# Finding the 896 unused rows and sending zeros to them, in place of zeroing all 39 blocks of the first layer's second group

## The reference, cut to what matters

```python
logits = jnp.einsum('btd,ed->bte', X, routing_W) + expert_bias      # 8 experts
activation = jnp.sqrt(jax.nn.softplus(logits))
top_vals, top_idx = jax.lax.top_k(activation, 2)
combine = jnp.sum(jax.nn.one_hot(top_idx, 8) * top_vals[..., None], axis=-2)
hdn = jax.nn.silu(jnp.einsum('nd,edh->enh', Xf, rW1) + rb1[:, None, :])
y = jnp.einsum('enh,ehd->end', hdn, rW2) + rb2[:, None, :]
routed = jnp.einsum('ne,end->nd', combine, y)
return shared + routed
```

## Time and profile before

| | us |
|---|---|
| median of 3 runs | 814.96 (814.42 to 817.94) |
| the profiled execution, its own time | 822.08 |
| its span | 820.2 |
| busy in the span: PE, DVE, ACT, POOL | 749.1, 530.4, 489.3, 429.7 |

### The profile page before, as it was taken

How to read it: one execution, slowest core, us unless ns; L and a number is a source line. 1 busy time by engine, 2 the same in 40 slices (tenths; PEclk the granted TensorE clock), 3 DMA queues, 4 the chain that set the end, 5 groups by cost and what they waited for, 6 DMA issues and landing times.

```text
span 820.2 us, 16199 instructions
## 1 busy us (share of the span) xinstructions
PE 749.1 (91%) x4633; PEld 653.7 (80%) x4633; DVE 530.4 (65%) x1423; ACT 489.3 (60%) x1379; POOL 429.7 (52%) x399
## 2 busy tenths in 40 slices
PE   4799987889898499999999999789999999999996
PEld 3546635676776399999998988689999999999995
DVE  5687857552665488888889888776543343365454
ACT  2337735555676488888877787356555454454541
POOL 3000655564687958888545778544652445333220
PEclk9899999999999799999999999899999999999998
DMA  8999997787899943663610444633444434565457
GB/s 248 343 285 308 332 300 257 241 276 227 184 268 241 320 121 81 163 153 70 210 63 2 161 163 148 206 104 120 140 137 142 144 104 133 179 210 177 161 178 233
DMA packets 128745, 154.47 MB, mean 188 GB/s; under 512 B 10875, under 2 KB 118550, under 8 KB 127638
## 3 DMA queue, kind: packets, MB, share of 16 engines
q1 hardware_dynamic: 102896, 112.55, 44.7%
q0 software_dynamic: 18624, 34.29, 15.8%
q10 hardware_dynamic: 7142, 6.59, 2.4%
HBM read 77.39 MB, written 76.00 MB: 187 GB/s over the span
## 4 chain that ended last, share of the span: by engine, by line
PE 70%; DVE 8%; issue 5%; ACT 5%; POOL 5%; DMA 4%; DVEq 1%; another core or an unknown queue 0%; SPq 0%; POOLq 0%; ACTq 0%
PE psum L849 24%; PE psum L1164 9%; PE psum L1142 8%; PE psum L1236 7%; PE psum L1241 6%; PE psum L1237 6%; POOL X L718 4%; PE psum L1152 3%; PE psum L1252 3%; ACT pr L1549 2%; PE psum L1215 2%; DMA X<-yl_dram,slots_y 1%; DMA yk_dram<-ys,L 1%; PE psum L1037 1%; PE psum L942 1%
## 5 line engine op out<-in xcount | busy, mean ns | idle before, releaser
L771 POOL DMA_INDIRECT yk_dram<-ys,L x52 | 53.6, 1031 | 136.2 <-ACT ys L1641 136.0
L718 POOL DMA_INDIRECT X<-yl_dram,slots_y x64 | 101.0, 1578 | 31.9 <-issue 14.2
L690 POOL DMA_INDIRECT xs_dram<-N,slots x64 | 65.9, 1029 | 97.0 <-DVEq L1943 58.4
L1549 ACT ACTIVATE pr<-psum,nmx 128x64 f32<-128x64 f32 x512 | 108.4, 365 | 6.8 <-DVE nmx L2314 6.6
L1236 PE MATMUL psum<-whi,xTh 128*128 x284 | 103.9, 366 | 3.4 <-ACT xTh L1603 2.4
L2410 DVE TENSOR_TENSOR hs<-psum,hs 128x384 f32<-128x384 f32 x71 | 39.7, 559 | 87.4 <-PE psum L1241 45.2
L1237 PE MATMUL psum<-wlo,xTh 128*128 x284 | 96.0, 338 | 0.0
L759 POOL DMA_INDIRECT xs_dram<-N,slots x64 | 69.7, 1090 | 35.9 <-ACT ys L1641 19.1
L1241 PE MATMUL psum<-whi,xTl 128*128 x284 | 74.1, 342 | 1.5 <-DVE xTl L2433 1.4
L751 POOL TENSOR_TENSOR pr<-pr,sm 128x1024 f32<-128x1024 f32 x32 | 62.2, 1944 | 19.5 <-DVE sm L2321 17.3
L1633 ACT ACTIVATE hs<-psum 128x384 f32<-128x384 f32 x71 | 34.9, 492 | 49.0 <-PE psum L1241 36.7
(11 more groups left out here) (370 smaller groups left out, 2041.2 us busy)
## 6 DMA issues: line engine op xcount, KB each, us to landing
fx<-xs_dram SPq DMA_DIRECT2D x78, 130.0 KB
yl_dram<-fy SPq DMA_DIRECT2D x78, 128.0 KB
xs_dram<-fill SPq DMA_DIRECT2D x4, 2340.0 KB, 14.1
xs<-xs_dram SPq DMA_DIRECT2D x71, 130.0 KB
wlo<-in_L_ffn_W_dram SPq DMA_DIRECT2D x4, 1536.0 KB, 11.4
xs_dram<-cz SPq DMA_DIRECT2D x1, 5070.0 KB, 24.2
xs_dram<-cz SPq DMA_DIRECT2D x7, 650.0 KB
X<-in_x_dram SPq DMA_DIRECT2D x4, 1024.0 KB, 11.7
```

What stands on the lines that cost most here:

```text
L690: po.indirect_dma_start(XS, bass.IndirectOffsetOnAxis(ap=slot[k][:, t:t + 1], axis=0), N0[:, t, :], None).then_inc(s[done], 16)
L718: po.indirect_dma_start(X[:, t, :], None, YL[b // 2], bass.IndirectOffsetOnAxis(ap=slot_y[k][:, t:t + 1], axis=0), compute_op=ALU.add).the ...
L771: po.indirect_dma_start(YK, bass.IndirectOffsetOnAxis(ap=yid[:, j:j + 1], axis=0), ys[j % YB], None).then_inc(s[f"y_out{j % YB}"], 16)
L1549: last = act(pr[b][:, S * h:S * h + S], bank[2 * b + h // 8][:, S * (h % 8):S * (h % 8) + S], ACT.Exp, bias=nmx[:, h:h + 1])
```

## The change

Group 1's rows are no longer filled. GpSimd writes the numbers 0, 128, ..., 768 plus the partition's into `pad_no` once, at the start. Behind `choose(1)` VectorE runs `padding()`, which finds for each of the 896 numbers which expert's open rows it falls to and writes the row in `pad_at`. Behind the 32 sends of group 1, GpSimd sends 128 rows of zeros 7 times by that list. SP waits for these too before it issues `vraw` and group 1's loads. The stores of `st_r` share semaphores two by two.

```diff
+PADS = LS - 2 * LT
@@ tiles
+        pad_no, pad_at = nmx[:, 0:PADS], sm[0][:, 0:PADS].bitcast(I32)
@@ SP
-            parts = [LS * i // PAIRS for i in range(PAIRS + 1)]
-            sp.dma_start(rows_of[0], zeros.to_broadcast([P, LS, XW])).then_inc(s["zeroed0"], 16)
+            sp.dma_start(XS[0:LS * P, :].rearrange("(p r) d -> p r d", p=P), zeros.to_broadcast([P, LS, XW])).then_inc(s["zeroed"], 16)
...
-                                     ...).then_inc(s[f"st_out{i}{j % DEEP}"], 16)
+                                     ...).then_inc(s[f"st_out{i // 2}{j % DEEP}"], 16)
-                sp.dma_start(rows_of[1][:, parts[j]:parts[j + 1], :],
-                             zeros.to_broadcast([P, parts[j + 1] - parts[j], XW])).then_inc(s["zeroed1"], 16)
...
                 if g:
+                    sp.wait_ge(s["padded"], 16 * PADS)
                     sp.dma_start(vraw, VD[0].rearrange("p (m c) n -> p m (c n)", c=2)).then_inc(s["v_in"], 16)
@@ GpSimd
+            po.iota(pad_no, pattern=[[P, PADS]], base=0, channel_multiplier=1, allow_small_or_imprecise_dtypes=True)
@@ GpSimd, send_rows(g)
-                po.wait_ge(s[f"zeroed{g}"], 16 * (1, PAIRS)[g])
+                if g == 0:
+                    po.wait_ge(s["zeroed"], 16)
...
+                if g:
+                    po.wait_ge(s["pads"], 1)
+                    for i in range(PADS):
+                        po.indirect_dma_start(
+                            XS, bass.IndirectOffsetOnAxis(ap=pad_at[:, i:i + 1], axis=0),
+                            zero4, None).then_inc(s["padded"], 16)
@@ VectorE, called between choose(1) and routed(0)
+            def padding():
+                base, e_ = LS * P, E * LT
+                counts, cum, open_, at = (ta[:, 2 * E * k:2 * E * k + E] for k in range(4))
+                at = at[:, 0:PADS]
+                c3 = wk12[:, 0:PADS * E].rearrange("p (i e) -> p i e", e=E)
+                last_t = tc_[:, e_:2 * e_].rearrange("p (e t) -> p e t", e=E)[:, :, LT - 1:LT]
+                nc.vector.tensor_copy(counts.rearrange("p (e a) -> p e a", a=1), last_t)
+                ve.drain()
+                nc.vector.tensor_tensor_scan(cum, ones8[:, :], counts, 0.0, ALU.mult, ALU.add)
+                ve.drain()
+                tt(cum, counts, cum, ALU.subtract)
+                ve.drain()
+                stt(open_, te[:, :], float(P), cum, ALU.mult, ALU.add)
+                ve.drain()
+                tt(c3, bc(pad_no, E), rep(open_, PADS), ALU.is_ge)
+                ve.drain()
+                tt(c3, c3, rep(counts, PADS), ALU.mult)
+                ve.drain()
+                nc.vector.tensor_reduce(at, c3, AX.X, ALU.add)
+                ve.drain()
+                stt(pad_at, at, float(base), pad_no, ALU.add, ALU.add)
+                ve.drain()
+                ve.sem_inc(s["pads"], 1)
@@
             choose(1)
+            padding()
             routed(0)
```

More of the change, by code:

```diff
@@ L307, in build @@
         VD = nc.dram_tensor("vw_dram", [NB, P, PAIRS, D], F32).ap()
-        names = """consts ctx_in u_in x_in0 x_in1 x_in2 x_in3 s_in0 s_in1 s_in2 s_in3 wq_in kvo_in w_in0 w_in1 w_in2 w_in3 w_hi w_lo cols_in rest_in cw_in l1_in zeroed0 zeroed1
+        names = """consts ctx_in u_in x_in0 x_in1 x_in2 x_in3 s_in0 s_in1 s_in2 s_in3 wq_in kvo_in w_in0 w_in1 w_in2 w_in3 w_hi w_lo cols_in rest_in cw_in l1_in zeroed pads padded
             u_c_in mid_in
-            pre_c_tp pre_c_sb wqt_p wqt_sb k_p k_sb v_p v_sb a_p vw_p st_sb st_out00 st_out01 st_out02 st_out10 st_out11 st_out12 st_out20 st_out21 st_out22 st_out30 st_out31 st_out32
+            pre_c_tp pre_c_sb wqt_p wqt_sb k_p k_sb v_p v_sb a_p vw_p st_sb st_out00 st_out01 st_out02 st_out10 st_out11 st_out12
             b2_in b2_lo b2_zero sw_in rw_in
@@ L416, in _ @@
             zeros = zero4[:, :].rearrange("p (a d) -> p a d", a=1)
-            rows_of = [XS[LS * P * g:LS * P * (g + 1), :].rearrange("(p r) d -> p r d", p=P) for g in range(LG)]
-            parts = [LS * i // PAIRS for i in range(PAIRS + 1)]
             sp.wait_ge(s["kvo_in"], 16 * 3)
@@ L438, in _ @@
                         sp.dma_start(AD[:, :, i, P * j:P * j + P].rearrange("b p n -> p b n"),
-                                     st_r[i][j % DEEP].rearrange("p (b n) -> p b n", b=NB)).then_inc(s[f"st_out{i}{j % DEEP}"], 16)
+                                     st_r[i][j % DEEP].rearrange("p (b n) -> p b n", b=NB)).then_inc(s[f"st_out{i // 2}{j % DEEP}"], 16)
                     else:
@@ L442, in _ @@
                         sp.dma_start(VD[2 * h:2 * h + 2, :, j, :].rearrange("b p n -> p b n"),
-                                     st_r[i][j % DEEP].rearrange("p (b n) -> p b n", b=2)).then_inc(s[f"st_out{i}{j % DEEP}"], 16)
-                sp.dma_start(rows_of[1][:, parts[j]:parts[j + 1], :],
-                             zeros.to_broadcast([P, parts[j + 1] - parts[j], XW])).then_inc(s["zeroed1"], 16)
-            for i in range(4):
+                                     st_r[i][j % DEEP].rearrange("p (b n) -> p b n", b=2)).then_inc(s[f"st_out{i // 2}{j % DEEP}"], 16)
+            for i in range(2):
                 for d in range(DEEP):
-                    sp.wait_ge(s[f"st_out{i}{d}"], 16 * len(range(d, PAIRS, DEEP)))
+                    sp.wait_ge(s[f"st_out{i}{d}"], 16 * 2 * len(range(d, PAIRS, DEEP)))
             for c in range(DC):
@@ L1382, in fold @@
                     if j >= DEEP:
-                        ac.wait_ge(s[f"st_out{i}{j % DEEP}"], 16 * (j // DEEP))
+                        ac.wait_ge(s[f"st_out{i // 2}{j % DEEP}"], 16 * 2 * (j // DEEP))
                     bk_, sc = (bank[2 + i], DH ** -0.5) if i < DC else (bank[3 + i], 1.0)
@@ L1424, in shared_out @@
                 elif q == 2:
-                    ac.wait_ge(s["st_out00"], 16 * len(range(0, PAIRS, DEEP)))
+                    ac.wait_ge(s["st_out00"], 16 * 2 * len(range(0, PAIRS, DEEP)))
                 for h, k in enumerate((6, (5, 4)[q // LQ])):
```

## The result

The changed kernel took 819.2 us (median of 20 runs), the kernel before 815.1 beside it. The ratio is 1.0058, with a 95% interval from 1.0037 to 1.0078: 4.7 us slower, 3.0 to 6.4. At 0.58% the slowdown lies just past the 0.5% up to which I had said "same" (chance 0.71), so in "slower" (0.23); its interval reaches to both sides of that line.

What follows compares the result with a forecast made beforehand. GpSimd's collects through `scale(0)` were taken as the bound. VectorE +1.03, GpSimd +1.35 and 0.2 for waits, with removal and SP at 0, made +2.6 us on 814.96: 817.6 us, range 812.5 to 821.0.

Steps and rivals of the forecast that it cites:

- Bound: GpSimd's collects of group 0 and `scale(0)`, 199.07 to 281.09 us, release TensorE's softmax turn; a late start ends late.
- Removal at 0: Dropping group 1's fill (5070 KB, 69 to 118 us) gains 0, since nobody on the chain waits for it.
- VectorE, +1.03: `padding()` ahead of `routed(0)` takes 2.12 us; block 0's copy, and the blocks' end, come 1.03 us later.
- The cover, TensorE's turn: VectorE's 1.09 us idle for TensorE's turn ahead of block 0's copy was to hide that much of `padding()`.
- GpSimd, +1.35: Seven sends behind group 1's last one take 8.82 us; what idle time doesn't cover delays the first collect by 1.35.
- the 7.78 idle us: GpSimd's idle time between its last send and the first collect, said to cover nearly all of the seven sends.
- slower collects: Rival: loads moving among the first eight collects lengthen two landing waits, 819.6 to 821.6 us; chance 0.15.
- SP's loads, 0: `vraw` goes out 7.1 us later, group 1's blocks start 1.0 to 4.0 us late; slack absorbs it, priced 0.
- this rival: Loads too late: group 1's late blocks use up the slack and GpSimd waits, 819.6 to 820.6 us; chance 0.08.
- the slack of 4.2: Group 1's blocks were done at about 262.8 us, 4.2 us before GpSimd passes their wait ahead of collect 33.
- Sum: Removal 0, VectorE +1.03, GpSimd +1.35 and 0.2 for waits, SP 0: +2.6 us, giving 817.6 us.

Runs made afterwards that it cites:

- run 1: Kernel before, fill kept, with `padding()` added ahead of `routed(0)` and its result unused: 1.0022, 817.88 us.
- run 9: Kernel before, unedited, measured again in a later batch: 1.0000, 813.77 us.
- Run 2: Kernel before, fill kept, no `padding()`, plus seven sends to spare rows that SP waits for and the shared semaphores: 1.0062, +5.1 us.
- run 4: Changed kernel, unedited, measured again in the batch of the first experiments: 1.0104 to the kernel before.
- run 3: Changed kernel with the eight fills of group 1 put back: 1.0109 to the kernel before.
- run 5: Kernel before, unedited, measured again as control in the batch where it took 829.35 us: 1.0019.
- run 6: Kernel before, fill kept, no `padding()`, seven sends to spare rows, shared semaphores, SP not waiting for the sends: 1.0106.
- run 11: Run 6 repeated in another batch (sends to spare rows, fill kept, SP not waiting): 1.0113 to the kernel before.
- run 7: Changed kernel with its seven sends spread behind every second send of group 1 from tile 21 on: 1.0148 to the kernel before.
- run 8: Run 7 with `padding()` also moved behind the copy of block 2 in `routed(0)`: 1.0207 to the kernel before.
- run 12: Run 8 repeated in another batch (sends in gaps, `padding()` behind block 2's copy): 1.0153 to the kernel before.
- run 10: Run 7 repeated in another batch (changed kernel, sends spread into gaps): 1.0040 to the kernel before.

## Why the prediction was right, and where its size was off

- **Bound.** Right. GpSimd's run from the first collect to `scale(0)` sets the softmax turn, and what starts it late ends it late. From the last result of group 0 on ScalarE to the first collect it is 3.1 us in runs 1 and 9 and 7.7 in all four executions with the pads in a row. Run 2, which delays nothing but that start and SP's loads, lost 5.1 us. Its time alone doesn't tell GpSimd's late start from SP's wait; its trace has no wait for group 1's blocks, and run 4, whose trace has one, lost 8.5 us beside it.
- **Removal at 0.** Right: runs 3 and 4, 1.0109 with and 1.0104 without the fill. The copies of the earlier trace rows don't stall in the changed kernel, but neither do they in runs 1, 2, 3 and 9, which keep the fill. And in the batches of 829 and 830 us they stall in every execution, with the fill (runs 5, 6, 11) and without it (runs 7, 8, 12): the fill is not what makes them late.
- **VectorE, +1.03.** The length was right (2.13 for 2.12). Of its effect the traces show less: from the first instruction of `choose(1)` to the copy of block 0 it is 17.94 us in run 9, 18.32 in the changed kernel (118.66 to 136.98) and 18.13 in run 1, so 0.2 to 0.4 more. The cover, TensorE's turn, was 1.62 us in run 9 and 1.09 in the execution that I read; 2.13 - 1.62 = 0.51. But in run 2, without `padding()`, TensorE's turn had begun at 136.41 and VectorE has no idle time ahead of the copy at all:

```profile
121.80 0.29 DVE L1934 TENSOR_TENSOR L<-psum,rb_bc 128x128 f32<-128x128 f32 x1 [4.37 <-PE psum L962]
...
138.02 0.40 DVE L2005 COPY fxT<-psum 128x256 f32<-128x256 f32 x1
```

That is 16.22 us, and in run 3, the same with `padding()` and the real rows, 18.17: 1.95 more, nearly the whole 2.13. So the cover is between 0 and 1.62 from one execution to the next. Nor does the copy alone set the start of the blocks: from `choose(1)` to ScalarE's first result it is 18.8, 20.9 and 23.3 us in three executions without `padding()` and 21.4 to 23.3 in five with it. The term stays unmeasured; the timed ratio of run 1, -0.2 to 3.8 us, holds all of this.

- **GpSimd, +1.35.** This is the step that was mis-sized: "the 7.78 idle us cover nearly all of the pads". The mechanism, each send's 1.26 and the idle time's place were right, and the cover was that of an execution with a stop in it. Measured: 11.05 to the first collect against 6.17 in run 9, so 4.88 in place of 1.35. Of the 3.53 between them 2.56 are the cover that was smaller (8.73 - 6.17), and 0.97 are the sends themselves: one of the seven took 1.89 and not 0.96 (1.90 in run 4, 1.55 in runs 2 and 3), with 0.04 in gaps and roundings.
- **Collects.** The rival "slower collects" falls, and the reverse is seen: in the four executions with the pads ahead of them the collects took 81.0 to 81.6 us (run 4's 85.2 less its wait of 3.69 is 81.5), where runs 9 and 1 took 83.1 and 83.5. The first collect lasts 1.74 in place of 2.45, and the landing waits are 7.1 to 7.9 in place of 8.4 and 8.6. That would be about 1.9 us given back. But two executions with no pads right ahead took 82.0 (the one that I predicted from, its first collect 1.72 long) and 82.1 (run 10), so what is shown is 0.4 to 2.5. I had this term at 0.
- **SP's loads, 0.** Right in three of four executions with the pads in a row, and by a hair. `vraw` went out 1.63 us behind the last pad, and TensorE waited 3.28 for the first block; VectorE's wait for the first additions (2.83 in run 9, 3.00 in the earlier trace rows) is gone in the changed kernel, as the cover that I had named. But run 4 passed the slack and GpSimd paid 3.69. I gave this rival 0.08, which is too little: the slack of 4.2 came from the same single execution. In the changed kernel collect 33 starts 3.25 us behind group 1's last result on ScalarE (261.39 to 264.64), and in run 3 3.48 with an idle time of 0.62 in place of 0.30, where group 0's results needed 3.09 in run 9; run 9 itself has 5.25 there, a slack of about 2.2. And run 5 shows that `routed_done(1)` can be late in the kernel before too (9.3 us waited for stored results in two waits, the first 7.0, so 2.3).
- **Sum.** By the traces, with run 9 for the kernel before: +0.4 on VectorE, +4.9 on GpSimd, -1.9 in the collects, and run 4's 3.7 in one execution of four, about 0.9: 4.3 us, against 4.7 (3.0 to 6.4) timed. That agreement is better than its terms: VectorE's may be 0.2 to 2.0, the collects' -0.4 to -2.5, and the share of one in four is a guess, since the three executions without the wait were 2.4 to 4.5 us faster than the median of their kernel, and run 4's was its median. Nor does the sum give the 8.5 and 8.9 us of runs 4 and 3. With the whole 3.7 it comes to 7.1, and the lower granted clock between 44 and 54 us, in some executions and not in others, can add some 3 (`choose(0)` at 66.6 to 67.2 us against 62.6 to 64.2). The forecast's 2.6 came out too low by the cover. That it lies as near as it does is in part luck: GpSimd's term was 3.5 too small, and the collects, taken at 0, gave some of that back.

Open stays what SP's wait costs by itself where there are no stalls (runs 6 and 11 both fell into batches that have them), how often the late loads hold GpSimd up, what the stalls are, and whether the lower clock from 44 to 54 us has to do with the change.

## What to carry to other kernels

Idle time that is to cover new work should be read from more than one execution, or at least checked for a stall just ahead of it: the earlier trace rows showed 7.78 us, two executions without a stop had 5.2 and 5.5, and the 3.3 us stop that made most of the difference stood in the same trace. The same goes for slack that is to absorb a late start: 4.2 there, about 2.2 in run 9. Work moved from a hardware queue's transfer (5 MB of zeros, which cost nothing where they were) to a slow issuer on the chain (seven sends at 1.26 us) is paid for by the issuer, not by the bytes. When the issuer is the bound, such sends can go into its earlier gaps, and then it takes more than one batch to judge: the same move came to 1.0040 in one and to 1.0148 in another, and in neither was it faster than the kernel before.

## What the runs showed of the hardware

- The same kernel took 815 us beside some batches and 829 to 830 beside others. Since two batches with the same chip number in the record differ so, the chip alone is not shown to be the reason. The profiled executions of runs 5 and 9 are 20.2 us apart (spans 832.1 and 811.9): 8.5 ahead of group 0's first result, with the stop of 4.29 in the scores; 6.7 in group 0's blocks (55.3 for 48.7), where 7.4 us are TensorE's waits ahead of products with `rw_sb`, of which run 9 has none; 1.4 in the collects; 3.7 behind them. The mean granted clock was 0.972 in run 5 and 0.979 in run 9.
- In these stops VectorE, ScalarE and TensorE are late together and GpSimd's transfers go on: in run 5 VectorE and ScalarE both start again at 110.99 us after 4.29 and 4.23 idle, with GpSimd sends at 107.30, 108.56 and 109.83.
- In these batches there were more such waits beside added sends: 14.0 and 14.6 us in runs 6 and 11, 11.8 and 14.1 in runs 7 and 12, and 7.4 in run 5 without them. One trace of the kernel before doesn't show that the sends are the cause.
- From 46 to 50 us the granted clock was 0.50 (1.2 GHz) in five of fourteen executions and 1.00 in the result's, with TensorE busy for all of 38 to 44 us at 1.00 in both. VectorE's `choose(0)` starts in the five at 66.6 to 67.2 us, in the other nine executions at 62.6 to 64.2.
- One send of seven, the fifth each time, lasts 1.55 to 1.90 us in place of 0.96, in the four executions with the pads in a row and no such waits; in runs 6 and 11 all seven last 0.96.
- The landing of a 128-row send was seen by SP within 1.63 us of the send's end in the changed kernel (196.98 to 198.61) and in run 4 within 1.87 (200.60 to 202.47), so 2.59 and 2.83 us behind its start. The Trainium skill, page "DMA: Bandwidth & Descriptors", section "Anatomy of one DMA — SWDGE (gpsimd) path", has a fixed part of about 2.0 us for setup and completion, which would be an estimate of 2.3 for these 130 KB. Counted from the send's end, as I did in the prediction, the loads would by that rule have gone out 0.4 to 0.7 us later than they did; counted from its start, 0.3 to 0.5 us earlier. The two traces lie to either side of the estimate, by where one starts the count.
